# A mixer and mixture-of-experts block on one core: the state update fused on VectorE, the skip products on ScalarE, the result's statistics later

## The reference, cut to what matters

```python
x_mlstm, z = split(x @ W_up);  x_act = swish(causal_conv(x_mlstm) + conv_b)
q, k, v = headwise(x_act, Wq), headwise(x_act, Wk), headwise(x_mlstm, Wv)   # 4 heads of 64
C = q @ k.T * DH**-0.5 * exp(logD - max(logD));  norm = max(|C.sum(-1)|, exp(-mD))
hn = headnorm((C / (norm + 1e-6)) @ v) * norm_w
mixer = ((hn + skip * x_act) * swish(z)) @ W_down
Y = layernorm(x + mixer)
g = sigmoid(Y @ gate_w.T);  combine = top 4 of g, divided by their sum
routed = sum_e (silu(Y @ e_win[e]) * (Y @ e_vin[e]) * combine[e]) @ e_wout[e]
shared = (silu(Y @ ws_in) * (Y @ vs_in)) @ ws_out
out = layernorm(Y + shared + routed)
```

## Time and profile before

| | |
|---|---|
| median of three executions | 886.41 us |
| the profiled execution: its own time | 881.61 us |
| its span, first to last instruction | 879.9 us |
| busy: PE, DVE, ACT, POOL | 90%, 75%, 41%, 42% |
| mean granted TensorE clock | 0.963 |

### The profile page before, as it was taken

One profiled execution on the slowest core, in us unless ns is written; L12 is line 12 of the kernel. 1 busy time (PEld: TensorE's weight loads), 2 busy tenths in 40 slices (PEclk: granted clock), 3 DMA queues, 4 the chain that ended last, 5 costly groups with the idle time before them and its releaser, 6 DMA issues.

```text
span 879.9 us, 17647 instructions
## 1 busy us (share of the span) xinstructions
PE 789.5 (90%) x5783; PEld 665.3 (76%) x5783; DVE 658.6 (75%) x1711; ACT 363.2 (41%) x621; POOL 372.1 (42%) x370
## 2 busy tenths in 40 slices
PE   6879967599999999999999999999999999999966
PEld 5656656488887888887878787878787878787855
DVE  5799953577777787777777777777777777778754
ACT  4757732234344344343343434343434343433231
POOL 5050018542635363636353545463535454544200
PEclk8999977689999999999999999999999999999979
DMA  4878744210404040404040404040403040400000
GB/s 119 242 244 278 272 164 129 95 49 25 131 24 131 24 131 24 131 24 131 24 131 24 132 24 131 24 131 24 131 24 131 24 131 24 131 24 25 1 12 13
DMA packets 53104, 81.01 MB, mean 92 GB/s; under 512 B 10176, under 2 KB 36952, under 8 KB 49112
## 3 DMA queue, kind: packets, MB, share of 16 engines
q1 hardware_dynamic: 53080, 80.68, 29.8%
HBM read 55.24 MB, written 25.43 MB: 92 GB/s over the span
## 4 chain that ended last, share of the span: by engine, by line
PE 38%; DVE 20%; issue 17%; DMA 11%; POOL 7%; SPq 2%; ACT 2%; POOLq 1%; DVEq 1%; ACTq 0%
DMA max_b<-max_scratch 11%; PE bank L1395 10%; PE bank L1366 5%; DVE acc L838 5%; PE bank L1370 4%; PE bank L1367 4%; PE bank L1339 3%; DVE st L990 3%; PE bank L1385 3%; DVE out_sb L1002 2%; POOL D L548 2%; POOL D L538 2%; DVE Y L1002 2%; POOL kept L567 2%; PE bank L1315 2%
## 5 line engine op out<-in xcount | busy, mean ns | idle before, releaser
L754 ACT ACTIVATE s_in<-bank 128x512 f32<-128x512 f32 x144 | 86.1, 598 | 178.5 <-PE bank L1370 177.6
L1395 PEld LDWEIGHTS bank<-ewout,h 128*128 128x128 f32 x1024 | 132.8, 191 | 8.6
L1366 PE MATMUL bank<-yT_hi,in_hi 128*128 128x512 f32 x288 | 128.8, 447 | 11.2 <-DVE h L1097 11.2
L552 POOL TENSOR_TENSOR rs<-ve,half 128x4 f32<-128x4 f32 x32 | 32.7, 1020 | 241.9 <-DVE ve L998 241.9
L1395 PE MATMUL bank<-ewout,h 128*128 128x128 f32 x1024 | 134.8, 275 | 0.0
L1097 DVE TENSOR_TENSOR h<-s_in,bank 128x512 f32<-128x512 f32 x144 | 98.1, 681 | 48.0 <-PE bank L1370 44.3
L538 POOL TENSOR_TENSOR D<-a_tok,max_b 128x512 f32<-128x512 f32 x64 | 65.5, 1044 | 120.4 <-DVE max_b L910 67.8
L1370 PE MATMUL bank<-yT_lo,in_hi 128*128 128x512 f32 x288 | 114.8, 398 | 0.0
L1367 PE MATMUL bank<-yT_hi,in_lo 128*128 128x512 f32 x288 | 114.4, 397 | 0.0
L1101 DVE TENSOR_TENSOR h<-h,bank 128x512 f32<-128x512 f32 x128 | 87.2, 681 | 14.4 <-PE bank L1385 14.4
L951 DVE TENSOR_TENSOR state<-kept,bank 64x130 f32<-64x130 f32 x128 | 36.6, 286 | 62.6 <-POOL kept L567 41.5
(11 more groups left out here) (193 smaller groups left out, 1643.7 us busy)
## 6 DMA issues: line engine op xcount, KB each, us to landing
xact_scratch<-xact SPq DMA_DIRECT2D x16, 1024.0 KB, 5.0
max_b<-max_scratch SPq DMA_DIRECT2D x15, 1024.0 KB, 7.6
xa<-xact_scratch SPq DMA_DIRECT2D x16, 512.0 KB, 6.4
silu_z<-xact_scratch SPq DMA_DIRECT2D x16, 512.0 KB, 3.7
inter_w<-inter_scratch SPq DMA_DIRECT2D x30, 256.0 KB, 7.5
x_in<-in_L_attn_x_dram SPq DMA_DIRECT2D x16, 256.0 KB, 4.8
xt_scratch<-x_t SPq DMA_DIRECT2D x16, 256.0 KB, 5.0
xT<-xt_scratch SPq DMA_DIRECT2D x16, 256.0 KB, 8.1
```

What stands on the lines that cost most here:

```text
L754: act.activation(s_in[:, j % 2], bank[4][:], ACT.Silu).then_inc(silu_done, 1)
L1366: pe.matmul(o, in_hi[:, m, j], yT_hi[:], start=True, stop=False)
L1395: i = pe.matmul(bank[7][:, k * P:(k + 1) * P], h2[:, j % 2, k * P:(k + 1) * P], w, start=(j == k == 0), stop=(j == NJ), skip_group_check=True)
```

## The change

The kept products and their tile go. VectorE's update multiplies and adds in one instruction, once for each pair of heads and parity (4 per chunk, where 2 additions stood). The skip products move from GpSimd to ScalarE, into slot 1. The statistics of the result (z2) are cut off from the sum and stand behind the next group's `mix_front` and `yT_low`, just ahead of `ffn_norm`. `mixer_norm` waits for z2_done, and VectorE waits once for the decays at its start.

```diff
             def mix(g, f):                      # GpSimd
-                dec = decay[:].rearrange("p s (g k) -> p g k s", k=NC)[:, bass.ds(g, 1)].rearrange("p g k s -> p (g k) s")
                 for k in range(NC):
-                    if k:
-                        pool.wait_ge(state_done[k - 1], g + 1)
-                    else:
-                        prev(pool, state_done[NC - 1], g)
-                    pool.tensor_tensor(kept[:], state[:], dec[:, k, :].unsqueeze(2).to_broadcast([P, NP, 2 * DV]),
-                                       ALU.mult).then_inc(kept_done[k], 1)
-                    if k == 0:
-                        prev(pool, down_mm, g)
-                        alone(pool)
-                    if k < NP:
-                        pool.tensor_scalar(mixed[:, k], xa[:, k], vecs[:, k, VS:VS + 1], None, ALU.mult
-                                           ).then_inc(skip_done, 1)
                     if k in (1, 2) and not (isinstance(g, int) and g == NG - 1):
                         args(g + 1, k - 1)
...
                 for j in range(NJ + 1):         # ScalarE, mix
                     if f is not None:
                         ffn_slot(f, j)
+                    if j == SKIP_SLOT:          # SKIP_SLOT = 1
+                        act.wait_ge(xa_in, 16 * (g + 1))
+                        prev(act, down_mm, g)
+                        for p in range(NP):
+                            act.activation(mixed[:, p], xa[:, p], ACT.Copy, scale=vecs[:, p, VS:VS + 1]
+                                           ).then_inc(skip_done, 1)
...
             def update_state(g, k):             # VectorE
                 dve.wait_ge(upd_mm[k], g + 1)
-                dve.wait_ge(kept_done[k], g + 1)
+                if k:
+                    dve.wait_ge(state_done[k - 1], g + 1)
+                else:
+                    prev(dve, state_done[NC - 1], g)
+                now = decay[:].rearrange("p s (g k) -> p g k s", k=NC)[:, bass.ds(g, 1), k].rearrange("p g s -> p (g s)")
                 new = bank[0][:, 0:NP * 2 * DV].rearrange("p (s d) -> p s d", s=NP)
                 for par in range(2):
                     r, c = slice(par * DH, (par + 1) * DH), slice(par * DV, (par + 1) * DV)
-                    i = dve.tensor_tensor(state[r, :, c], kept[r, :, c], new[r, :, c], ALU.add)
+                    for s in range(NP):
+                        i = dve.scalar_tensor_tensor(state[r, s, c], state[r, s, c], now[r, s:s + 1], new[r, s, c],
+                                                     ALU.mult, ALU.add)
...
             def mixer_norm(g):
                 dve.wait_ge(rs1_done, g + 1)
+                dve.wait_ge(z2_done, g + 1)
                 normalise(Y, y1, mv1, rs1, Y_done)
...
                     mix_front(g + 1)
                 yT_low(g)
                 if f is not None:
+                    ffn_statistics(f)
                     ffn_norm(f)
...
                 dve.tensor_tensor(flat(z2), bank[7][:], flat(Y), ALU.add).then_inc(z2_done, 1)
+
+            def ffn_statistics(f):
                 dve.wait_ge(z2_done, f + 2)
                 statistics(f, z2, st2, mv2, ve2, st2_done, mv2_done, ve2_done)
...
                 ffn_sum(f)                      # VectorE, the last group's ffn
+                ffn_statistics(f)
                 ffn_norm(f)
...
             dve.wait_ge(phase2_const, 5)
+            dve.wait_ge(decay_in, 16 * 2 * NP)
```

More of the change, by code:

```diff
@@ L153, in mixer_moe_block @@
         state = sb("state", [P, NP, 2 * DV])
-        kept = sb("kept", [P, NP, 2 * DV])
         p1 = ExitStack()
@@ L286, in mixer_moe_block @@
         u_mm, u_out = sems("u_mm", NC), sems("u_out", NC)
-        upd_mm, kept_done, state_done = sems("upd_mm", NC), sems("kept_done", NC), sems("state_done", NC)
+        upd_mm, state_done = sems("upd_mm", NC), sems("state_done", NC)
         sq_done, ssq_done = sem("sq_done"), sem("ssq_done")
@@ L1486 @@
             3: (("S", 3),), 4: (("R", 1),), 6: (("H", None),)}
+SKIP_SLOT = 1
 U_SLOT = {0: 0, 1: 1, 2: 2, 3: 3}
```

## The result

The change makes the kernel slower: 934.0 us (median of 4, 931.59 to 941.33) against 888.4 us for the kernel before in the same series, ratio 1.053 (95% interval 1.045 to 1.061). The profiled execution has a span of 932.3 us against 879.9, 52.4 us more. I had forecast 946 us from a range of 908 to 965, +65 us on the profiled execution.

The account below looks back on a forecast made before the run. TensorE, busy 95% of the steady loop, was taken to bound the kernel. Lateness of 58.8 less 13.7 gave +45.1 on 881.6, 926.7 us; the clock's 19.6 made 946 us, range 908 to 965.

Parts of the forecast that it names:

- gap before chunk 0: TensorE, before the matmul on state and qs: a gap of 3.9 us, 3.5 us late, waiting for qs.
- out_sb's four beside qs: VectorE, at the group border: four out_sb instructions beside GpSimd's qs take 3.15 us, between 1.11 and 3.86.
- fused update: VectorE's state update: four instructions of 64x65 take 0.9 us instead of 0.58, +0.3.
- The mechanism: GpSimd, group border: power then qs, behind statistics that follow yT_lo; qs ends at 495.04 instead of 490.23.
- The clock term: TensorE, after the gap: granted clock falls to half speed, 1.4 us a group, 14 x 1.4 = 19.6 us.
- The cover: TensorE before chunk 1: 1.5 us of half-speed time is free, since TensorE would have waited for VectorE.
- The slowdown under it: TensorE from chunk 0 to chunk 1: half speed doubles chunk 0 and ffn_in, 3.2 us more at most.
- kept's wait: TensorE, ffn_in's second half, waiting for h: 12 gaps of 1.14 us go, 13.7 us won.
- the head scale: VectorE, between update and h: starts earlier; kept's gain holds if it clears TensorE, each tenth short costs 1.4 us.
- The DMA queue: Store of out_sb, x_res, max_b: out_done and argument work 3.45 us later, cost nil; up to 0.4 us a group otherwise.
- One sign: VectorE, in the changed profile: no idle time in front of the third update.
- chunk 1's lateness: TensorE, chunk 1: starts at 500.0 instead of 495.81, 4.2 us late in 14 groups, 58.8 us.

Follow-up runs that it names:

- e1: The changed kernel with the result's statistics back ahead of Y; fused update and skip products on ScalarE stay; 869.9 us, 0.980 of the kernel before.
- e2: The kernel before with only the result's statistics moved behind yT_low; kept and GpSimd's skip products stay; 947.8 us, 1.071 of the kernel before.
- e8: The changed kernel with the next group's qs formed right behind hn on GpSimd, where it stands idle; 910.3 us, 1.032 of the kernel before.
- e3: The changed kernel with GpSimd's order turned, qs ahead of the power for the result; 930.3 us, 1.048 of the kernel before.
- e4: The changed kernel with four unused fp32 matmuls on TensorE before the first chunk of every group but the first; 936.9 us, 1.056 of the kernel before.
- e9: The kernel of e6 with the four unused matmuls of e4 in the gap; 901.5 us, 1.019 of the kernel before.
- e6: The changed kernel with out_sb moved to slot 2 a group later and its store behind the loads; 932.8 us, 1.055 of the kernel before.
- e7: The changed kernel with qs early, result's statistics in slot 2, out_sb in slot 9 a group later, power behind the argument work, store last; 852.2 us, 0.964 of before.

## Why the prediction was right, and where it was off

Measured from the group's first keys matmul (482.80 before, 650.24 after), by its own steps:

| step | predicted | measured |
|---|---|---|
| Y starts | 2.8 | 2.76 |
| statistics end, power starts | 8.86 | 8.73 |
| qs ends | 12.24 | 12.04 |
| gap before chunk 0 | 3.9 | 3.61 |
| out_sb's four beside qs | 3.15 | 3.03 |
| fused update | 0.9 | 0.97 |
| chunk 1 starts (13.01 before) | 17.2 | 17.03 in nine groups, 18.06 on average in five |

**The mechanism** is the one forecast: GpSimd's order (power, then qs) behind statistics that were moved past yT_lo. e1 and e2 show that the moved statistics are the cause, e8 that 24 us of it go once qs is out of the queue and meets neither Y nor out_sb; what stays is VectorE's statistics and its wait for the power. The row that gave the contention was a single one in the trace of before; e3 and e8 confirm it from both sides.

**The clock term was mis-sized.** I took 1.4 us a group, 19.6 us, on top. The clock did fall in all 14 groups: for 3.4 us in nine, for 6.8 us in five. In the nine, chunk 1 started 4.9 us after chunk 0 at either clock (662.38 to 667.27 after; 666.60 to 671.53 in e4), because VectorE's update ended only then, and the loss fitted under that wait. In the five, matmuls at half speed made the update's operand and ffn_in late enough to show: chunk 1 started 5.8 to 6.1 us after chunk 0, 1.0 us later than in the nine. TensorE, kernel after, one of the five, where the update ended at 474.70:

```profile
469.78 0.77 PE L1317 MATMUL bank<-state,qs 128*128 128x130 f32 x2 [3.60 <-issue]
...
472.39 1.18 PE L1324 MATMUL bank<-vals,keys 128*128 128x130 f32 x4
...
475.53 0.39 PE L1317 MATMUL bank<-state,qs 128*128 128x130 f32 x2
```

So the clock cost 5 us in the kernel after, and not 19.6; e4 confirms it, where chunk 1 is at 17.02 in every group. The cover was about what I had allowed (e4 waits 1.28 us for the update, I had 1.5). The slowdown under it was not: I had put up to 3.2 us there, and from chunk 0 to chunk 1 it is 1.3 us with a short stretch (3.30 us in e9, 4.59 in e6's one group) and 2.4 with a long one (5.69).

**The gain of kept's wait was somewhat oversized.** Chunk 1 was 4.02 us late (17.03 less 13.01) in 14 groups, 56.3 us, and 5 us more by the clock in five; the groups grew by 14 x 3.66 = 51.2. So about 10 us came back behind chunk 1, of the 13.7 that I had counted: from chunk 1 to the next group's first matmul 31.24 us before and 30.49 after. The sum held only if the head scale cleared TensorE, and it does not: GpSimd's argument work runs beside it. It did so in the kernel before as well:

```profile
506.80 0.87 DVE L961 SCALAR_TENSOR_TENSOR nrm<-nrm,floor_tok 128x8 f32<-128x8 f32 x1
```

```profile
505.60 2.04 POOL L538 TENSOR_TENSOR D<-a_tok,max_b 128x512 f32<-128x512 f32 x2
```

VectorE's timeline, kernel after, another group:

```profile
628.24 0.97 DVE L948 SCALAR_TENSOR_TENSOR state<-state,decay,bank 64x65 f32<-64x65 f32 x4 [1.67 <-PE bank L1324]
629.24 0.90 DVE L957 SCALAR_TENSOR_TENSOR nrm<-u_sb 128x8 f32<-128x8 f32 x1
630.27 0.87 DVE L959 SCALAR_TENSOR_TENSOR nrm<-nrm,floor_tok 128x8 f32<-128x8 f32 x1
```

GpSimd, the same stretch:

```profile
625.88 2.04 POOL L537 TENSOR_TENSOR D<-a_tok,max_b 128x512 f32<-128x512 f32 x2 [11.38 <-DMA max_b<-max_scratch]
627.88 1.23 POOL L547 TENSOR_SCALAR_AFFINE_SELECT D<-D 128x512 f32<-128x512 f32 x2
629.08 2.04 POOL L537 TENSOR_TENSOR D<-a_tok,max_b 128x512 f32<-128x512 f32 x2
```

GpSimd waits for max_b, and its two products of 1.02 us from 629.08 lie over the two nrm, which take 0.90 and 0.87 us; alone each takes 0.17. The head scale of a group has eight instructions of this size, which together take 2.88 us in the kernel before, 2.64 on average in the kernel after, and 1.36 in e6, where the argument work lies elsewhere; there it is 29.95 us from chunk 1 to the next group, so about 0.5 us a group, 7 us, were still to be had.

The DMA queue cost nothing, as I had said. The argument work starts 3.7 us later in its group (22.9 us for 19.2 on average; I had 3.45), which is less than chunk 1's own lateness, and the head transposes waited 0.6 us in all for hn. One sign did not come: VectorE still stands idle 1.67 us in front of the third update (628.24 above), now for TensorE's product and no longer for kept.

**Term by term**, predicted and measured: chunk 1's lateness 58.8 and 56.3, kept's wait -13.7 and about -10, the clock 19.6 and 5; together 64.7 and 51, while the profiled execution grew by 52.4 (881.6 to 934.0). The forecast of 946 was 12 us too high: the clock made it 14.5 too high and the lateness 2.5, and kept's term took some 3.5 back. The last us or two are not accounted for. What I had not seen is that fused update and skip products are worth 2% by themselves (e1), about a third of it ahead of chunk 1, where out_sb no longer runs beside them; in the kernel after that part shows only as out_sb's 3.03 us where e2 has 3.75.

The Trainium skill, page "GPSIMD Engine Reference", section "8. Key points", says that GpSimd shares its SBUF interfaces with VectorE and gets in the way of instructions in a two-port mode or with two SBUF inputs. The runs agree for nrm (two inputs), which went from 0.17 to 0.90 us. out_sb and Y have one tensor input and were slowed too, out_sb's four from 1.12 to 3.03 us; that fits if they run in a two-port mode, which no run here shows.

## What to carry to other kernels

Before moving a step on one engine, follow what it releases on the others to the end of their queues: here 1.7 us of statistics, moved to win 0.4 us, dragged a power and, behind it in a fixed order, the operand of the next chunk. If an instruction is to leave the path, move its whole chain (statistics, power, normalisation) into slots where each engine is idle, as e7 does. And read two engines side by side: work taken off GpSimd may pay on VectorE, and two delays of the same length hide each other, so that testing them one at a time shows next to nothing. Then read the group's own time beside the total: six executions of e1 lie between 862.9 and 874.2 us, further apart than such a part is worth.

## What the hardware showed that I had not expected

- The granted clock fell also after gaps of 1.8 us and shorter: e8 has 7 stretches at 0.50 in its loop, with no gap above 1.82 us before the keys products and 1.3 before chunk 1, while the kernel before, with single gaps of 1 us, has none.
- Four fp32 matmuls whose results are thrown away kept the grant at 1.00 through the whole loop (e4, e9).
- A VectorE instruction of 340 ns that starts just behind GpSimd's qs (2.34 to 2.37 us) takes up to 2.37 us in the kernel before; the four of out_sb took 3.03 us in the kernel after, the longest single one 2.26 us, as if the first ended only with qs.
